# Three of the last mixture's four experts computed inside the attention's maxima pass, with the pass itself, list D and layer 0's edge terms rebuilt

## The chip, the cores and the metric

The kernel runs on one core of one Trainium2 chip. The metric is the device time of the execution in microseconds (us), the median of several runs. The core has five engines with a queue of instructions each: TensorE (PE; PEld is its weight load), VectorE (DVE), ScalarE (ACT), GpSimd (POOL) and SyncE (SP), which here only issues transfers. They wait for each other through semaphores.

## The reference, cut

Four stages on 6,250 nodes with 256 features, each added to its own input after a layer norm: a graph sum over 100,000 edges with a dense pair of layers, a mixture of eight experts, five graph layers with batch norm, and a last mixture of four experts whose shares come from graph attention. The change is about the last one.

```python
h = (x_flat @ W_gat).reshape(M, HEADS, NUM_EXPERTS)       # M = 6250 rows (the norm's batch is 1), 4 heads, 4 experts
src = concatenate([edge_index[0], loops]); dst = concatenate([edge_index[1], loops])   # 65,536 edges and a self loop each
a_src = (h * att_src).sum(-1);  a_dst = (h * att_dst).sum(-1)
e = leaky_relu(a_src[src] + a_dst[dst], 0.2)
ee = exp(e - segment_max(e, dst)[dst])
alpha = ee / (segment_sum(ee, dst)[dst] + 1e-16)
agg = segment_sum(h[src] * alpha[:, :, None], dst) + b_gat
scores = layernorm(agg).reshape(M, HEADS, NUM_EXPERTS).mean(1);  topk_s, topk_i = top_k(scores, 2)
for ei in range(NUM_EXPERTS):                              # every expert on every node, 256 -> 512 -> 256
    hh = gelu(x @ W1[ei] + b1[ei])
    out = out + g[..., None] * (hh @ W2[ei] + b2[ei])      # g: softmax weight where chosen, else 0
```

An expert's product needs no attention; only its share g does.

## The kernel before

Nodes are 49 tiles of 128 rows, in 7 groups of 7 tiles. The work is a list of phases, each ended by a barrier. The setup phase sorts three lists of edges by target tile on VectorE: A (first graph sum), C (the layers) and D (attention). List D has E2T = 561 columns of 128 edges, 512 of the 65,536 edges and 49 of self loops. A list is placed into DRAM by GpSimd's indirect scatters (L260), one a column. After placement the edges lie in chunks of 128 with one target tile each: NC2 = 624 for list D.

*The layers.* Five times, GpSimd gathers source rows with an indirect DMA for each chunk (L305), TensorE multiplies them with a one-hot matrix (L390), VectorE adds the bank to the tile's sum (L376). Behind its gathers of each layer GpSimd places a part of list D: 130 columns before the layers, 58 in each of layers 0 to 3, and the 199 that are left in layer 4. Layer 0 then adds the edges' own features for each of 14 half tiles: four f32 matmuls of 448 columns into the pair of banks own (L959), which wait until VectorE has added the pair before (L1012). The last layer's statistics end at L1053, and the barrier comes when GpSimd too is done.

*The last norm* (L618 to L671). Seven groups: load, normalise, turn to feature-major with TensorE, multiply with W_gat, copy the product (L647). SP first issues list D's load, then the norm's transfers.

*Attention*, first pass, the maxima. The table nodesD has 20 words a node: a_src of 4 heads and h. It is stored from row, and then 39 turns of 4 sets of 4 chunks run. For a set: ScalarE copies the indices (L1182), GpSimd gathers four times 128 rows (L305), ScalarE keeps them and makes 16 matrices of 128 by 128 with a_src on the diagonal (L1178), VectorE makes four matrices that hold a not-equal mask of the target (cold, L1277). TensorE writes, for each chunk, the row values spread over all partitions (ones times diag, f32, 512 columns, L1218) and minus 1e30 where the target differs (bf16, L1220) into a bank of 512 columns. Eight banks hold two sets. VectorE reduces four banks with one operation (L1288) and takes the maximum into the window's tile (L1295). TensorE is behind VectorE by its banks (the semaphore reduced). The second pass, the sums, takes the same rows from SBUF in 78 steps of 8 chunks. It gathers nothing.

*The last mixture* (class Ffn, also used for the first dense stage and the first mixture). The four experts' weights are loaded at its start, in about 10 us. For each group and expert TensorE makes 8 banks of up projections (L472, 32 matmuls), ScalarE the gelu (L506), TensorE 7 tiles of down projections (L485, 56 records), and VectorE adds the bias and the product, each times its share, to acc (L523, L527). Between two groups SP stores acc, waits for the store, and loads the next group's base into it:

```python
sp.wait_ge(self.stored, START + g * 16)
sp.dma_start(self.acc, group_rows(self.base, g)).then_inc(self.base_here, 16)
```

TensorE may run two experts ahead by its two hidden buffers, but only four tiles ahead by its y banks. With a single expert there is one hidden buffer.

## Time and profile before

| what | value |
|---|---|
| median of 3 runs | 15026.75 us (15017.78 to 15076.48) |
| the profiled execution, its own time | 15050.61 us |
| its span | 15048.9 us |
| granted TensorE clock, mean | 0.754 |
| busy: TensorE, weight load | 7919.9 us (53%), 5777.6 us (38%) |
| busy: VectorE, GpSimd, ScalarE | 6704.7 us (45%), 7539.6 us (50%), 1802.1 us (12%) |
| layers | 5110 to 12521 us |
| seam and last norm | 12521 to 12790 us |
| attention: start, maxima, sums, shares | 12797, 12826 to 13805, 13811 to 14330, to 14354 us |
| last mixture's experts | 14354 to 15049 us |

Times of stages are positions in the profiled execution, read off the timeline. Busy time is what an engine executes; the rest of its span it waits. The granted clock is a share of full speed: 0.50 is 1.2 GHz and 1.00 is 2.4 GHz.

### The profile page before, as it was taken

How to read it: one execution, taken by the hardware profiler on the slowest of the kernel's cores; microseconds unless marked ns; L12 is line 12 of the kernel's file. 1: busy time of each engine (PE TensorE's matmuls, PEld its weight loads, DVE VectorE, ACT ScalarE, POOL GpSimd, SP SyncE). 2: the span in 40 equal slices, each digit the busy share in tenths (PEclk: the TensorE clock that was granted, in tenths of full speed). 3: DMA queues.
4: the chain of work that ended last, by engine and by line, in shares of the span. 5: the costliest groups of instructions: out<-in, count | busy, mean ns of one | idle time of the engine just before them, and what ended most of it. 6: DMA issues, size and time to landing. Idle time of an engine off the chain costs nothing. (4 is left out here: it accounts for less than half of the span.)

```text
span 15048.9 us, 161728 instructions
## 1 busy us (share of the span) xinstructions
PE 7919.9 (53%) x35664; PEld 5777.6 (38%) x35704; DVE 6704.7 (45%) x18970; ACT 1802.1 (12%) x5161; POOL 7539.6 (50%) x7803
## 2 busy tenths in 40 slices
PE   0002455442139777656554655565556542676489
PEld 0002344331126544435443544444434442233356
DVE  7238544311015555544443444344434442566732
ACT  0000000000001100010001000100010001786211
POOL 5771566535750155545665666566656664563000
PEclk9999766675569888867666766677777665898599
DMA  1000222211000223213332333233323321100000
GB/s 56 18 1 0 76 85 85 71 43 43 2 6 20 84 80 80 80 56 85 86 86 70 86 86 87 69 86 86 86 68 85 86 75 36 8 7 4 0 30 17
DMA packets 483984, 833.28 MB, mean 55 GB/s; under 512 B 182276, under 2 KB 320821, under 8 KB 482869
## 3 DMA queue, kind: packets, MB, share of 16 engines
q0 software_dynamic: 327584, 673.89, 17.2%
q1 hardware_dynamic: 156309, 158.42, 3.3%
q8 instruction: 27, 0.44, 0.0%
q14 instruction: 64, 0.52, 0.0%
HBM read 751.88 MB, written 86.32 MB: 56 GB/s over the span
## 5 line engine op out<-in xcount | busy, mean ns | idle before, releaser
L305 POOL DMA_INDIRECT p_layers_place<-nodesC,p_layers_idx x4160 | 3945.7, 948 | 3033.1 <-issue 1593.1
L390 PE MATMUL p_layers_bank<-p_layers_hots,p_layers_place 128*128 128x128 f32 x16640 | 3440.7, 367 | 2872.0 <-DVE agg L376 1579.2
L390 PEld LDWEIGHTS p_layers_bank<-p_layers_hots,p_layers_place 128*128 128x128 f32 x16640 | 2927.3, 261 | 3471.1 <-issue 1858.6
L376 DVE TENSOR_TENSOR agg<-agg,p_layers_bank 128x256 f32 x4160 | 1752.1, 421 | 2445.0 <-issue 1052.1
L366 DVE TENSOR_SCALAR p_layers_hots<-iota,p_msg_edges 128x128 f32<-128x128 f32 x3328 | 995.7, 364 | 758.9 <-issue 581.9
L485 PE MATMUL p_ffn_y<-p_ffn_w,p_ffn_hid 128*128 128x256 f32 x3528 | 832.5, 396 | 724.0 <-issue 691.9
L305 POOL DMA_INDIRECT p_gather_rows<-xn,p_gather_idx x832 | 788.1, 947 | 838.3 <-ACT p_gather_idx L299 603.2
L260 POOL DMA_INDIRECT listC<-h x782 | 783.2, 1002 | 582.5 <-POOLq L1518 243.2
L485 PEld LDWEIGHTS p_ffn_y<-p_ffn_w,p_ffn_hid 128*128 128x128 f32 x3528 | 693.9, 198 | 874.6 <-issue 747.9
L260 POOL DMA_INDIRECT listA<-h x782 | 853.5, 1091 | 343.9 <-issue 238.8
L390 PE MATMUL p_agg_bank<-p_agg_hot,p_gather_rows 128*128 128x128 f32 x3328 | 695.0, 378 | 602.0 <-DVE agg L376 384.2
L299 ACT COPY p_layers_idx<-p_msg_edges 128x4 int32 x1040 | 203.1, 197 | 6418.2 <-PE p_layers_bank L390 2923.4
L390 PEld LDWEIGHTS p_agg_bank<-p_agg_hot,p_gather_rows 128*128 128x128 f32 x3328 | 611.6, 275 | 685.7 <-issue 448.1
L305 POOL DMA_INDIRECT gat_att_rows<-nodesD,gat_att_idx x624 | 590.9, 947 | 552.9 <-issue 183.7
L1218 PE MATMUL gat_att_banks<-gat_att_diag,ones 128*128 128x512 f32 x1248 | 709.2, 652 | 247.1 <-issue 127.8
L1178 ACT ACTIVATE gat_att_diag<-ident,gat_att_rows 128x128 f32<-128x128 f32 x2496 | 766.5, 388 | 166.7 <-issue 126.1
L260 POOL DMA_INDIRECT listD<-recD,rowD x561 | 552.9, 986 | 174.2 <-issue 174.2
L527 DVE SCALAR_TENSOR_TENSOR p_ffn_acc<-p_ffn_y,p_mix_share,p_ffn_acc 128x256 f32<-128x256 f32 x392 | 189.4, 483 | 960.3 <-remote 702.5
L376 DVE TENSOR_TENSOR agg<-agg,p_agg_bank 128x256 f32 x832 | 350.4, 421 | 454.2 <-issue 218.5
L472 PE MATMUL p_ffn_pre<-agg,p_ffn_w 128*128 x1120 | 454.8, 560 | 126.5 <-ACT p_ffn_hid L506 58.4
L506 ACT ACTIVATE p_ffn_hid<-p_ffn_pre,p_ffn_b 128x896 f32<-128x896 f32 x252 | 253.7, 1007 | 2150.5 <-PE p_ffn_pre L472 1025.8
L1288 DVE TENSOR_REDUCE gat_att_red<-gat_att_banks 128x16 f32<-128x2048 f32 x156 | 356.8, 2287 | 241.4 <-PE gat_att_banks L1220 101.4
(334 smaller groups left out, 7757.8 us busy)
## 6 DMA issues: line engine op xcount, KB each, us to landing
p_layers_place<-nodesC,p_layers_idx POOLq DMA_INDIRECT x4160
nodesC<-p_layers_place SPq DMA_DIRECT2D x24, 896.0 KB, 4.2
p_gather_rows<-xn,p_gather_idx POOLq DMA_INDIRECT x832
p_ffn_acc<-x SPq DMA_DIRECT2D x14, 896.0 KB, 5.2
x<-p_ffn_acc SPq DMA_DIRECT2D x14, 896.0 KB, 4.1
listA<-h POOLq DMA_INDIRECT x782
listC<-h POOLq DMA_INDIRECT x782
gat_att_rows<-nodesD,gat_att_idx POOLq DMA_INDIRECT x624
```

The source lines that it names most:

```text
L260: nc.gpsimd.indirect_dma_start(out=self.table, out_offset=bass.IndirectOffsetOnAxis(ap=self.row[0:n, t:t + 1], axis=0), in_=self.rec[0:n, ...
L299: nc.scalar.copy(self.idx[s], nodes).then_inc(self.ready[s], 1)
L305: nc.gpsimd.indirect_dma_start(out=self.rows[s][:, u, :], out_offset=None, in_=self.table, in_offset=bass.IndirectOffsetOnAxis(ap=self.idx ...
L366: ins = nc.vector.tensor_scalar(self.hot[s][:, u, :], self.sh.iota, place, weight, ALU.is_equal, ALU.mult)
L376: nc.vector.tensor_tensor(to, to, prod, ALU.add).then_inc(self.added[u], 1)
L390: ins = nc.tensor.matmul(self.bank[u][:, f * P:(f + 1) * P], self.g.rows[s][:, u, f * P:(f + 1) * P], self.hot[s][:, u, :], start=True, st ...
L472: ins = nc.tensor.matmul(self.pre[j][:, m, 0:HW], self.w1[:, e, f, b * P:(b + 1) * P], self.tok[:, f, ds(g * GW + m * HW, HW)], start=(f = ...
L485: ins = nc.tensor.matmul(self.y[j][:, 0:D], self.hid[e % self.nh][:, b, s * P:(s + 1) * P], self.w2[:, e * HB + b, :], start=(b == 0), sto ...
L506: nc.scalar.activation(self.hid[e % nh][:, b, :].rearrange("p (m n) -> p m n", m=2), self.pre[b % 2][:, :, 0:HW], self.func, bias=self.b1[ ...
L1178: ins = nc.scalar.activation(self.diag[s][:, u, a, :], sh.ident, ACT.Copy, scale=self.g.rows[s][:, u, a:a + 1])
L1218: nc.tensor.matmul(bank, sh.ones, self.diag[s][:, u].rearrange("p a n -> p (a n)"), start=True, stop=False)
L1288: nc.vector.tensor_reduce(red, self.banks[s % 2].rearrange("p u (a n) -> p u a n", a=HEADS), AX.X, ALU.max).then_inc(self.reduced, 1)
```

## The change

1. **Self loops leave list D.** E2T becomes 512 and NC2 560, so the maxima pass has 140 sets instead of 156 and the sums pass 70 steps instead of 78. The maxima start from each node's own a_src, and the sums from the self loop's exponential and its product with h, in a few whole-width operations ahead of the sums pass (one of them on ScalarE).
2. **Layer 0's edge terms** go into six single banks (the pair own, and four that the sums used), each with its own count, and VectorE adds one bank at a time.
3. **List D's tail.** The scatters left after layer 3, now 150 (512 less 130 less 4 times 58), leave layer 4 and run on GpSimd in the phase of the last norm. SP there loads the weights of three experts first (six loads of 512 KB), then serves the norm, and only then, when GpSimd has signalled the list, loads list D.
4. **The maxima pass** (class Tail instead of Attention). A table row has 26 words instead of 20: behind a_src and h stand three bf16 parts of a_src, which VectorE makes in four operations before the store. ScalarE copies a set's parts (thirds), TensorE turns them with one matmul of 128 columns against the identity into 48 rows, ScalarE writes them out by head in four operations (spreads), and for each chunk TensorE multiplies a selector with them: two bf16 matmuls of 512 columns a chunk, no f32 one. The 16 diagonal matrices a set are gone. The banks for it are 2 instead of 8, so VectorE reduces one chunk at a time, with a maximum for each.
5. **Three experts beside it.** The pass has 7 outer turns of 20 sets, one for each group of nodes. In a turn the 45 units of three experts (8 half banks of up projection and 7 tiles of down projection each) are dealt out to the 20 sets, 2, 2, 2 or 3 each. TensorE's order in a set is chunks 0 and 1, a unit, the turning of the next set, chunks 2 and 3, the other units. ScalarE does the gelu of each up unit and the copy of each down unit to keep; SP stores keep into part_y in DRAM. The bias b2 comes in by a bf16 matmul of three parts.
6. **The last mixture** computes one expert. At each group SP loads, behind the base, the three stored parts (896 KB each), and VectorE adds each of them times its share, tile by tile, before the expert's own sums.

```diff
-E2T = E2 // P + NT
+E2T = E2 // P
...
+TRI = 3 * HEADS
+GAW = AW + TRI // 2
+PAD_D = 24
...
-NC2 = chunks_of(E2 + NP)
+NC2 = chunks_of(E2)
...
+        self.old = [sp.sb(f"old{n}", [P, GT, D]) for n in range(len(parts))]
...
+            for old, (table, _) in zip(self.old, self.parts):
+                sp.dma_start(old, group_rows(table, g)).then_inc(self.base_here, 16)
...
-            dve.wait_ge(self.base_here, (g + 1) * 16)
+            dve.wait_ge(self.base_here, (g + 1) * (16 * (1 + len(self.parts))))
+            for n, (_, weight) in enumerate(self.parts):
+                for s in range(GT):
+                    a = self.acc[:, s, :]
+                    if n:
+                        dve.wait_ge(self.part_added, START + (g * len(self.parts) + n - 1) * GT + s + 1)
+                    nc.vector.scalar_tensor_tensor(a, self.old[n][:, s, :], weight[:, ds(g * GT + s, 1), 0], a,
+                                                   ALU.mult, ALU.add).then_inc(self.part_added, 1)
             for e in range(E):
...
+        self.edge_banks = [self.own[:, o, 0:HW] for o in range(FB)] + [bank[:, 0:HW] for bank in self.a.bank]
...
-            end = min(self.scat.T, at + PER_D) if l + 1 < LAYERS else self.scat.T
-            self.scat.pool(nc, pool, at, end)
-            at = end
-        self.scat.pool_done(pool)
+            if l + 1 < LAYERS:
+                self.scat.pool(nc, pool, at, at + PER_D)
...
         def edge(m):
-            pe.wait_ge(self.own_added, START + self.TILES + m)
             for o in range(FB):
-                ins = nc.tensor.matmul(self.own[:, o, 0:HW], self.ewm[:, o * P:(o + 1) * P],
-                                       self.agge[:, m * HW:(m + 1) * HW], start=True, stop=True)
-            ins.then_inc(self.own_done, 1)
+                n = m * FB + o
+                if n >= len(self.edge_banks):
+                    pe.wait_ge(self.edge_joined, START + n + 1 - len(self.edge_banks))
+                nc.tensor.matmul(self.edge_banks[n % len(self.edge_banks)], self.ewm[:, o * P:(o + 1) * P],
+                                 self.agge[:, m * HW:(m + 1) * HW], start=True, stop=True).then_inc(self.edge_made, 1)
...
+class Tail:
...
+    EARLY = 3
+    HB = 4
+    SETS = NC2 // U
+    PER = SETS // NG
+    UP, DOWN = 2 * HB, GT
+    UNIT = UP + DOWN
...
+        self.bank = [sp.ps(f"bank{h}", [P, 512]) for h in range(2)]
+        self.tr = sp.ps("tr", [P, 512])
+        self.pre = [sp.ps(f"pre{h}", [P, 512]) for h in range(2)]
+        self.y = [sp.ps(f"y{h}", [P, 512]) for h in range(2)]
...
+    def pieces(self, j):
+        total = self.EARLY * self.UNIT
+        return [divmod(n, self.UNIT) for n in range(j * total // self.PER, (j + 1) * total // self.PER)]
...
+        with sp.Fori(0, NG) as g:
+            for e in range(self.EARLY):
+                sp.wait_ge(self.y_kept, START + (self.unit(g, e) + 1) * GT)
+                hold(sp)
+                sp.dma_start(group_rows(self.ys[e], g), self.keep).then_inc(self.y_stored, 16)
+        sp.wait_ge(self.y_stored, START + NG * self.EARLY * 16)
...
+        def arrived(g, j):
+            k = g * self.PER + j
+            act.wait_ge(self.tr_done, START + k + 1)
+            act.wait_ge(self.spread, START + (k - 1) * U if not isinstance(k, int) or k else START)
+            for a in range(HEADS):
+                ins = nc.scalar.activation(self.spreads[j % 2][:, a, :], self.tr[0:self.R, 0:P], ACT.Copy,
+                                           scale=self.of_head[:, a:a + 1])
+            ins.then_inc(self.spread_ready, 1)
+        def lift(g, j):
+            k, s = g * self.PER + j, j % S
+            self.landed(act, g, j)
+            hold(act)
+            nc.scalar.copy(self.thirds[j % 2], self.rows[s][:, :, AW:GAW].bitcast(BF16)).then_inc(self.lifted, 1)
+            nc.scalar.copy(self.all[:, ds(k * U, U), :], self.rows[s][:, :, 0:AW]).then_inc(self.kept, 1)
+            nc.scalar.copy(self.idx[s], nodes((k + S) * U)).then_inc(self.ready[s], 1)
+        def experts(g, j):
+            for e, n in self.pieces(j):
+                at = self.unit(g, e)
+                if n < self.UP:
+                    b, m = divmod(n, 2)
+                    if n == 0:
+                        act.wait_ge(self.y_done, START + at * GT)
+                    act.wait_ge(self.pre_done, START + at * self.UP + n + 1)
+                    nc.scalar.activation(self.hid[:, b, m * HW:(m + 1) * HW], self.pre[n % 2][:, 0:HW], ACT.Gelu,
+                                         bias=self.b1[:, e * self.HB + b:e * self.HB + b + 1]).then_inc(self.gelu_done, 1)
+                else:
+                    t = n - self.UP
+                    if t == 0:
+                        act.wait_ge(self.y_stored, START + at * 16)
+                    act.wait_ge(self.y_done, START + at * GT + t + 1)
+                    nc.scalar.copy(self.keep[:, t, :], self.y[t % 2][:, 0:D]).then_inc(self.y_kept, 1)
...
+        def turn(g, last):
+            for j in range(self.PER):
+                if not (last and j + 1 == self.PER):
+                    arrived(g, j + 1)
+                experts(g, j)
+                if not last or j + 2 < self.PER:
+                    lift(g, j + 2)
...
+        def turn_rows(g, j):
+            k = g * self.PER + j
+            pe.wait_ge(self.lifted, START + k + 1)
+            if not isinstance(k, int) or k:
+                pe.wait_ge(self.spread_ready, START + k)
+            nc.tensor.matmul(self.tr[0:self.R, 0:P], self.thirds[j % 2].rearrange("p u w -> p (u w)"), self.ident,
+                             start=True, stop=True).then_inc(self.tr_done, 1)
+        def chunk(g, j, u):
+            k = g * self.PER + j
+            if u == 0:
+                pe.wait_ge(self.cold_ready, START + k + 1)
+                pe.wait_ge(self.spread_ready, START + k + 1)
+            pe.wait_ge(self.reduced, START + k * U + u)
+            bank = self.bank[u % 2]
+            nc.tensor.matmul(bank, self.cold[j % 2][:, u, :], self.off.rearrange("p a n -> p (a n)"), start=True,
+                             stop=False)
+            nc.tensor.matmul(bank, self.sel[:, u, :], self.spreads[j % 2].rearrange("p a n -> p (a n)"), start=False,
+                             stop=True).then_inc(self.spread, 1)
+        def up(g, e, n):
+            at, (b, m) = self.unit(g, e), divmod(n, 2)
+            if n == 0:
+                pe.wait_ge(self.gelu_done, START + at * self.UP)
+            else:
+                pe.wait_ge(self.gelu_done, START + at * self.UP + max(0, n - 1))
+            for f in range(FB):
+                ins = nc.tensor.matmul(self.pre[n % 2][:, 0:HW], self.w1[e][:, f, b * P:(b + 1) * P],
+                                       sh.h[:, f, ds(g * GW + m * HW, HW)], start=(f == 0), stop=(f == FB - 1))
+            ins.then_inc(self.pre_done, 1)
+        def down(g, e, t):
+            at = self.unit(g, e)
+            if t == 0:
+                pe.wait_ge(self.gelu_done, START + (at + 1) * self.UP)
+            pe.wait_ge(self.y_kept, START + at * GT + max(0, t - 1))
+            y = self.y[t % 2][:, 0:D]
+            nc.tensor.matmul(y, self.ones3, self.b2s[:, e, :], start=True, stop=False)
+            for b in range(self.HB):
+                ins = nc.tensor.matmul(y, self.hid[:, b, t * P:(t + 1) * P], self.w2[e][:, b, :], start=False,
+                                       stop=(b == self.HB - 1))
+            ins.then_inc(self.y_done, 1)
...
+        def turn(g, last):
+            for j in range(self.PER):
+                some = self.pieces(j)
+                chunk(g, j, 0)
+                chunk(g, j, 1)
+                for e, n in some[:1]:
+                    piece(g, e, n)
+                if not (last and j + 1 == self.PER):
+                    turn_rows(g, j + 1)
+                chunk(g, j, 2)
+                chunk(g, j, 3)
+                for e, n in some[1:]:
...
+        thirds = self.row[:, :, AW:GAW].bitcast(BF16)
+        link(nc.vector.tensor_copy(thirds[:, :, 0:HEADS], source))
+        link(nc.vector.tensor_tensor(rest, source, thirds[:, :, 0:HEADS], ALU.subtract))
+        link(nc.vector.tensor_copy(thirds[:, :, HEADS:2 * HEADS], rest))
+        nc.vector.tensor_tensor(thirds[:, :, 2 * HEADS:TRI], rest, thirds[:, :, HEADS:2 * HEADS],
+                                ALU.subtract).then_inc(self.rows_ready, 1)
...
+        def largest(g, j, last):
+            k = g * self.PER + j
+            if not last:
+                matrices(g, j + 1)
+            red = self.red[j % 2]
+            windows = windows_of(nc, mybir.EngineType.DVE, self.cw, k * U, U)
+            for u, w in enumerate(windows):
+                dve.wait_ge(self.spread, START + k * U + u + 1)
+                nc.vector.tensor_reduce(red[:, u, :], self.bank[u % 2].rearrange("p (a n) -> p a n", a=HEADS), AX.X,
                                         ALU.max).then_inc(self.reduced, 1)
-                windows = windows_of(nc, mybir.EngineType.DVE, self.cw, c, U)
-                dve.wait_ge(self.reduced, START + k + 3)
-                for u, w in enumerate(windows):
-                    dve.wait_ge(self.maxed, START + c + u)
...
+        dve.wait_ge(self.self_ex, START + 1)
+        nc.vector.tensor_copy(self.sums[:, :, 0:HEADS], self.low)
+        wide = self.low.rearrange("p t (a o) -> p t a o", o=1).to_broadcast([P, NT, HEADS, XD])
+        link(nc.vector.tensor_tensor(by_head(self.sums[:, :, HEADS:AW]), by_head(self.h16), wide, ALU.mult))
+        dve.wait_ge(self.kept, START + self.SETS)
...
+                            for e in range(Tail.EARLY):
+                                sp.dma_start(w1[e], L1_ffn_W1[e].rearrange("(f p) h -> p f h", p=P)).then_inc(here, 16)
+                                sp.dma_start(w2[e], L1_ffn_W2[e].rearrange("(b p) d -> p b d", p=P)).then_inc(here, 16)
+                            norm.sp(nc, sp)
+                            sp.wait_ge(listed, START + 1)
+                            hold(sp)
                             sp.dma_start(edges[:, 0:NC2, :].rearrange("p c w -> p (c w)"),
-                                         lanes(listD)).then_inc(here, 16)
-                            norm.sp(nc, sp)
...
+                            scatD.pool(nc, pool, PART_D + (LAYERS - 1) * PER_D, E2T)
+                            scatD.pool_done(pool)
+                            nc.gpsimd.sem_inc(listed, 1)
...
+            ffn = Ffn(space("ffn"), sh, sh.h, XD - Tail.EARLY, 4, L1_ffn_W1[late], L1_ffn_b1[late], L1_ffn_W2[late],
+                      L1_ffn_b2[late], ACT.Gelu, share[:, :, late], x3, out,
+                      parts=[(parts_y[e], share[:, :, e:e + 1]) for e in range(Tail.EARLY)])
```

## Rows read from the trace of the kernel before

**Rows 1.** Windows: length, PE/PEld/DVE/ACT/POOL busy (instructions), granted clock, DMA share, GB/s.
```profile
12826.00:13805.00 979.00, 766.84 (x1833) 312.44 (x1872) 596.24 (x1392) 790.82 (x2792) 582.37 (x615) 0.91 0.09 7
13811.00:14330.00 519.00, 216.50 (x3120) 175.00 (x3120) 373.75 (x1944) 146.89 (x195) 0.00 (x0) 0.50 0.00 0
14354.00:15048.00 694.00, 677.09 (x2464) 468.83 (x2464) 172.26 (x392) 121.77 (x119) 0.00 (x0) 0.99 0.08 25
```

**Rows 2.** Chain of waits, last stage: start, us, work.
```profile
14389.78 12.09 PE p_ffn_y L485 x56
14401.86 12.03 PE p_ffn_pre L472 x32
```

**Rows 3.** Groups by line and form, the maxima pass, largest first.
```profile
L1218 PE MATMUL gat_att_banks<-gat_att_diag,ones 128*128 128x512 f32 x1248 | 709.2, 652 | 247.1 <-issue 127.8 <-DVE gat_att_cold L1277 61.7 <-ACT gat_att_diag L1178 54.2
L305 POOL DMA_INDIRECT gat_att_rows<-nodesD,gat_att_idx x624 | 590.9, 947 | 552.9 <-issue 183.7 <-DMA nodesD<-gat_att_row 179.8 <-ACT gat_att_idx L1182 137.6
...
L1288 DVE TENSOR_REDUCE gat_att_red<-gat_att_banks 128x16 f32<-128x2048 f32 x156 | 356.8, 2287 | 241.4 <-PE gat_att_banks L1220 101.4 <-remote 90.0 <-issue 49.1
...
L1277 DVE TENSOR_SCALAR gat_att_cold<-iota,gat_in_edges 128x128 bf16<-128x128 f32 x624 | 146.2, 307 | 60.9 <-issue 53.1 <-DVE gat_att_sums L1270 0.2
...
L1295 DVE TENSOR_TENSOR gat_att_top<-gat_att_top,gat_att_red 128x4 f32 x624 | 102.9, 165 | 100.4 <-DVE gat_att_red L1288 12.3 <-issue 10.5
```

**Rows 4.** Line L305: min/median/max ns, first to last start.
```profile
L305 POOL DMA_INDIRECT p_gather_rows<-xn,p_gather_idx x832: 940/947/1018, 1561.7 to 2843.4; - x167
...
L305 POOL DMA_INDIRECT gat_att_rows<-nodesD,gat_att_idx x624: 939/945/1032, 12814.9 to 13778.0; - x156
```

**Rows 5.** Window of layer 0.
```profile
5175.00:6535.00 1360.00, 983.82 (x4981) 610.48 (x4979) 803.63 (x3466) 39.96 (x203) 774.15 (x814) 0.82 0.30 80
```

**Rows 6.** Timeline of GpSimd and VectorE, end of layer 4.
```profile
12367.75 1.00 POOL L260 DMA_INDIRECT listD<-recD,rowD  x1 [0.30 <-issue]
...
12492.65 0.42 DVE L376 TENSOR_TENSOR agg<-agg,p_layers_bank 128x256 f32 x1 [10.78 <-remote]
...
12521.30 0.16 DVE L1053 TENSOR_TENSOR shift<-p_layers_bn_b,p_layers_part 128x2 f32<-128x2 f32 x1 [0.55 <-DVE p_layers_part L1052]
...
12618.18 1.09 POOL L260 DMA_INDIRECT listD<-recD,rowD  x1 [0.30 <-issue]
12635.01 0.12 POOL L1886 MEMSET gat_in_edges<- 128x32 int32 x1 [15.73 <-POOLq L1841]
```

**Rows 7.** Timeline of VectorE, last two groups of the last norm.
```profile
12771.07 0.28 DVE L647 COPY gat_in_h<-gat_norm_prod 128x112 f32 x1 [7.24 <-PE gat_norm_prod L671]
...
12790.37 0.27 DVE L647 COPY gat_in_h<-gat_norm_prod 128x112 f32<-128x112 f32 x1 [7.13 <-PE gat_norm_prod L671]
```

**Rows 8.** Timeline of VectorE, first mixture's norm.
```profile
3550.64 0.22 DVE L647 COPY mix_router_logits<-mix_norm_prod 128x56 f32 x1 [96.92 <-remote]
...
3564.45 0.22 DVE L647 COPY mix_router_logits<-mix_norm_prod 128x56 f32 x1 [5.32 <-PE mix_norm_prod L671]
```

**Rows 9.** Window of the sort of list D.
```profile
1383.20:1548.60 165.40, 1.41 (x6) 1.16 (x6) 159.92 (x262) 0.00 (x0) 0.00 (x0) 1.00 0.00 0
```

**Rows 10.** Timeline of TensorE, layer 0's edge terms.
```profile
6680.45 3.35 PE L959 MATMUL p_layers_own<-rows,p_layers_ewm 4*128 4x448 f32 x4 [1.25 <-DVE agg L1012]
```

**Rows 11.** Timeline of TensorE, maxima pass.
```profile
12900.37 0.38 PE L1220 MATMUL gat_att_banks<-gat_att_off,gat_att_cold 128*128 128x512 bf16 x1
...
12900.58 1.02 PE L1218 MATMUL gat_att_banks<-gat_att_diag,ones 128*128 128x512 f32 x2
```

**Rows 12.** Timeline of TensorE, first dense stage, after a wait.
```profile
3204.12 8.69 PE L472 MATMUL p_ffn_pre<-agg,p_ffn_w 128*128 x16 [58.39 <-ACT p_ffn_hid L506]
```

**Rows 13.** Timeline of VectorE and SP, last stage, between two groups.
```profile
14462.22 0.48 DVE L527 SCALAR_TENSOR_TENSOR p_ffn_acc<-p_ffn_y,p_gat_share,p_ffn_acc 128x256 f32<-128x256 f32 x1 [0.85 <-PE p_ffn_y L485]
...
14467.29 0.39 SPq L444 DMA_DIRECT2D p_ffn_acc<-x  x1
...
14472.29 0.48 DVE L523 SCALAR_TENSOR_TENSOR p_ffn_acc<-p_ffn_b,p_gat_share,p_ffn_acc 128x256 f32<-128x256 f32 x1 [9.59 <-DMA p_ffn_acc<-x]
```

More of the change, by code:

```diff
@@ L1184, in keep_turned @@
+        turn(NG - 1, True)
+        act.wait_ge(self.self_low, START + 1)
+        nc.scalar.activation(self.low, self.low, ACT.Exp).then_inc(self.self_ex, 1)
         def keep_turned(k, h):
@@ new lines, in piece @@
+        def piece(g, e, n):
+            if n < self.UP:
+                up(g, e, n)
+            else:
+                down(g, e, n - self.UP)
+        def turn(g, last):
[10 more added lines that the diff above has]
+                for e, n in some[1:]:
+                    piece(g, e, n)
@@ L1224, in look_up @@
+        pe.wait_ge(self.consts, START + 3)
+        turn_rows(0, 0)
+        with pe.Fori(0, NG - 1) as g:
+            turn(g, False)
+        turn(NG - 1, True)
         def look_up(k, h):
@@ L1300, in dve @@
+        matrices(0, 0)
+        with dve.Fori(0, NG - 1) as g:
+            for j in range(self.PER):
+                largest(g, j, False)
+        for j in range(self.PER):
+            largest(NG - 1, j, j + 1 == self.PER)
         dve.wait_ge(self.maxed, START + NC2)
```

259 lines of the change are left out of this document (157 added, 102 removed).

## The prediction

> **What bounds the kernel now.** I read the busy shares by stage first. The end of the kernel is three stages: the maxima pass, 979 us at a granted clock of 0.91; the sums pass, 519 us at 0.50; the last mixture's experts, 694 us at 0.99 [rows 1]. In the last stage TensorE is busy 677 of 694 us, and the chain of waits alternates 12.03 us of up and 12.09 us of down projections without a gap: 24.12 us for one expert on one group, 28 such units, so 675 us [rows 2]. It is plain arithmetic, and TensorE bounds it.
>
> The maxima pass has no such owner. Of its 979 us TensorE is busy 767, ScalarE 791, VectorE 596, GpSimd 582 [rows 1], for 156 sets of four chunks: 6.28 us a set. The groups by line show what fills it [rows 3]: GpSimd issues four gathers at 0.95 us and 0.30 us between two (183.7 us of "issue" before 624), 5.0 us a set; no engine needs more than that on its own. What holds it is seen in the gathers' first and last start: 624 in 963 us is 1.546 us each, and the first aggregation, with rows of 1 KB and quite other engines' work, has 832 in 1282 us, 1.542 us [rows 4]. Two passes that share nothing but the indirect gathers run at one pace, a quarter above what GpSimd alone would take. Layer 0, whose TensorE and VectorE have the most to do per chunk, runs at 1.67 us (814 in 1360 us) [rows 5].
>
> Then the seam between the layers and the last mixture. GpSimd's last 199 list D scatters run from 12367.8 to 12618.2, 1.26 us each. Beside them VectorE's adds come every 11.2 us, each after 10.78 us idle, where they came at the gathers' pace before; the layer ends at 12521.3, and all wait for GpSimd until 12635.0 [rows 6]. The norm behind it needs 19.3 us a group undisturbed [rows 7]. The first mixture's norm, which has scatters beside it, shows what scatters do to it: 96.9 us idle before one copy, and 13.8 us for the next group once they were over [rows 8].
>
> **Part by part.** The sum is made against the profiled execution, 15050.6 us for a span of 15048.9; the median of the runs is 15026.75, 24 us (0.16%) lower, so the sum's difference is taken off the median.
>
> *Sort D.* From 1383.2 to 1548.6 only VectorE works, 159.9 us of it on 561 columns [rows 9]. 512 columns are 8.7% fewer. If all were per column that is 14 us, if nothing 0; I take -13.
>
> *Edge terms of layer 0.* TensorE 3.35 us and 1.25 us of waiting for VectorE, 4.60 us for each of 14 tiles [rows 10]. With more banks the wait goes. Records overlap a little, so I take 3.1 us a tile, -21 (3.35 gives -17; VectorE's two adds and two statistics, about half of 4.6, give -31).
>
> *List D's tail beside the norm.* Twelve adds at 11.2 us become twelve at the gathers' 1.55, so the last add moves from 12492.7 to about 12386; the 28.6 us to 12521.3, part of it held too, shrink to some 23: 12409. GpSimd starts 150 scatters (512 less the 362 placed by then) at 12411 and issues for 189 us, to 12600, and I give 11 us for landing. The norm starts meanwhile (19 us after GpSimd, as 7 x 19.3 back from 12790.4 gives 12655 against 12635; now behind 3 MB of weights) and is held: one group took 96.9 us and more in [rows 8], so 1.5 groups. The other 5.5 cost 106 us: 12717. List D's load, now behind the norm on SP, adds 6: 12723 against 12790. -67. Bounds: no group gets through, -38; the norm not held at all, end at 12617, -173. Its price without cover is thus the 189 us of issue.
>
> *Attention's start.* Four thirds operations, selectors and flags before the table store: +4 (0 to +8). What prepares the biases lies beside the store and the first gathers.
>
> *The maxima pass.* 140 sets now. TensorE per set: eight bf16 matmuls of 512 columns at 0.21 us (12900.37 to 12900.58, [rows 11]) make 1.7 us, the turning of the thirds 0.05, and 21 units of 24.12 us [rows 2] plus 7 bias matmuls of about 0.11 spread over 140 sets 3.7 us: 5.5 us at the higher clock, for some 23 matmul records a set instead of 12. VectorE: the reduction of 2287 ns becomes four of about 0.62 (a quarter, and a fixed part), with four maxima at 0.27 apart, four matrices at 0.22 and register loads: 5.0 us. ScalarE gives up 16 copies a set and takes four short ones, two evacuations and 2.25 pieces of the experts; it comes off the path. GpSimd stays at 5.0. Two chunks, a piece, two chunks, the rest is the order on TensorE; a piece of 1.5 to 1.8 us covers two reductions (1.3 us), so the pair of banks costs little. The gathers' own pace gives 6.2 us a set: the floor. The other end is 8.0: the dispatch of every engine is slowed while indirect DMAs run (the 10.78 us of [rows 6] is its extreme), and TensorE has twice the records. Layer 0's 6.67 is the nearest row, since there too TensorE is fullest. I take 6.7: 938 us, -41 (-111 at 6.2; +141 at 8.0). If TensorE waits and its clock sags to 0.91 as now [rows 1], 5.5 becomes 6.0, still inside.
>
> *The sums pass.* The self loops' exponentials and product ahead of it +4. 70 steps instead of 78 at 519/78 = 6.65 us: -53. Nothing in a step changes.
>
> *The last stage.* 694 us become seven groups of one expert. TensorE needs 24.1 us a group, but the group's chain is now longer. Now: last add at 14462.2, store, load at 14467.3, first add of the next at 14472.3, 10.1 us [rows 13]. Three more loads of 896 KB stand behind the first, which all must have landed: the first took 5.0 us from issue; I give the others 3.3 each (an estimate, two thirds of that, since four queued loads share the setting up), so 20.1 us from the last add. Then 21 operations of 0.48 us [rows 13], started 0.40 apart since they overlap, add the stored experts, 8.4; four waiting sums, then TensorE's last three tiles at 1.73 us (12.09 over 7), 6.8 in all: 35.3 us. TensorE waits some 10 us in each, and comes back slow: after a wait, 16 matmuls took 8.69 us [rows 12] where half of 12.03 would be 6.0. With part of those 2.7 us, 37 us a group. First group 37, six more 222, end 8: 267 us, -427. Bounds: loads hidden, TensorE's 24.1 and 1.4 for the last activation, 25.5 a group, -499; loads one after another at 5 us each and the full 2.7, 43 a group, -391.
>
> The Trainium skill, "TensorE: Matmul & The Clock Gate", section "HAM oscillation — how this bites in real kernels", says that waits for DMA between short bursts drop TensorE to the low clock again and again. The burst in [rows 12] agrees in kind. By the rule the clock drops at every group, 2.7 us at most each as that row has it, which would make the sum 7 us larger.
>
> Sum: -13 -21 -67 +4 -41 +4 -53 -427 = -614. 15026.75 - 614 = 14413 us.
>
> **Rivals.**
> *The gathers set the pace* (20%): 6.2 us a set, -111 instead of -41, and a norm that is held less, some -40 more. 14413 - 110 = about 14300. For it: two passes at one pace [rows 4]. Against: layer 0 [rows 5].
> *Dispatch holds the maxima pass* (20%): 8.0 us a set or more, because long unrolled bodies and twice the records are read while gathers run. +182: about 14595. For it: [rows 5, 6]. Against: TensorE streams the last stage's bodies without a gap [rows 2]. The Trainium skill, "Runtime: NRT & Kernel Launch", section "Instruction fetch mechanics", says that a taken branch to instructions no longer held costs a stall. By it each of the few jumps back would stall; no row here prices one.
> *The last stage stays at the low clock* (9%): TensorE needs 48 us a group, 7 x 48 + 17 = 353, +86: about 14500. For it: the 10 us waits; the sums pass stays at 0.50 [rows 1]. Against: the burst after each wait is 19 us long.
> *Slower* (4%): one mechanism, experts' matmuls at the low clock for the whole maxima pass. 5.5 us become 11.0, and with the quarter that the gathers' neighbourhood costs 12 to 13 us a set: 12.5 x 140 = 1750, +812 on the forecast, 15225. It decides from 11.1 us a set on (6.7 + 614/140). Against: the clock is 0.91 in this pass at 78% busy, and the share rises.
> *No effect that can be told* (2%): a set between 10.6 and 11.1 us.
>
> **Numbers.** Forecast 45%, with 14340 to 14490 as its own range; gathers' pace 20%, dispatch 20%, low clock 9%, slower 4%, none 2%. A measurement of this kernel can tell about 0.5% (75 us) from no change. Range 14250 to 14630: it takes the first rival whole, with the better bounds of the norm and the last stage, and the second with 0.2 us a set more. Faster 94%, same 2%, slower 4%.
>
> **What would show it.** Right: the last stage near 267 us with VectorE waiting for the loads at each group; the maxima pass near 940 us, GpSimd at about 1.65 us a gather, clock above 0.9; the norm's groups stretched to near 100 us until the scatters end, then 19.3 us; the sums pass at 465 us; edge tiles 3.1 us apart. Wrong: gathers more than 2 us apart, last-stage groups not near 37 us, or a norm that runs on beside the scatters. The estimate stands or falls with the set time of the maxima pass, 140 us for each microsecond.

## The result

The changed kernel took 14470.85 us, median of 4 runs (14433.16 to 14485.11), beside 15022.26 us for the kernel before: a ratio of 0.962 (95% interval 0.9604 to 0.9635), 551 us less. The forecast was 614 less, 14413 us, with 14250 to 14630 as the range. The profiled executions differ by more, 15048.9 against 14431.4, 617.5 us; the table shows where most of the other 66 come from.

| from, to | before | after | difference | forecast |
|---|---|---|---|---|
| list D's sort, first operation to last | 166.8 | 154.9 | -12 | -13 |
| layer 0's last gather to its shift | 156.9 | 137.0 | -20 | -21 |
| that shift to the last gather of layer 4 | 5672.8 | 5626.1 | -47 | 0 |
| last gather of the layers to the norm's last copy | 423.9 | 340.8 | -83 | -67 |
| to the attention's first gather | 24.5 | 30.6 | +6 | +4 |
| first gather to the last maximum | 992.7 | 1015.2 | +23 | -41 |
| last maximum to the last sum | 524.6 | 474.4 | -50 | +4 -53 |
| last sum to the end | 716.7 | 279.2 | -438 | -427 |

These are first and last starts of the lines concerned (in the first row, to the end of the last operation), in the one profiled execution of each kernel.

The windows of the same three stages after, the kinds of column as in [rows 1]:

```profile
12663.00:13678.00 1015.00, 961.91 (x3180) 459.61 (x3244) 543.99 (x1673) 369.95 (x1305) 528.89 (x560) 0.98 0.16 26
13693.00:14155.00 462.00, 191.26 (x2783) 155.01 (x2781) 335.73 (x1732) 86.94 (x139) 0.00 (x0) 0.50 0.00 0
14183.00:14431.00 248.00, 187.40 (x616) 125.97 (x616) 101.76 (x245) 37.19 (x35) 0.00 (x0) 0.89 0.40 127
```

TensorE is now the owner of the maxima pass: 962 of 1015 us at 0.98, where it had 767 of 979 in [rows 1], a window that starts 11 us behind the first gather. That is 6.9 us a set of 140; I had summed 5.5. The timeline of TensorE there shows the difference:

```profile
13101.46 0.39 PE L1362 MATMUL gat_att_bank<-gat_att_spreads,gat_att_sel 48*128 48x512 bf16 x1
13101.78 0.39 PE L1360 MATMUL gat_att_bank<-gat_att_off,gat_att_cold 128*128 128x512 bf16 x1
13102.10 0.39 PE L1362 MATMUL gat_att_bank<-gat_att_spreads,gat_att_sel 48*128 48x512 bf16 x1
13102.42 0.28 PE L1382 MATMUL gat_att_y<-gat_att_b2s,gat_att_ones 3*128 3x256 bf16 x1
13102.63 1.99 PE L1384 MATMUL gat_att_y<-gat_in_w,rows 128*128 128x256 f32 x8
13104.55 0.24 PE L1350 MATMUL gat_att_tr<-gat_att_ident,gat_att_thirds 128*48 128x128 bf16 x1
13104.72 0.39 PE L1360 MATMUL gat_att_bank<-gat_att_off,gat_att_cold 128*128 128x512 bf16 x1
```

The bf16 matmuls of 512 columns start 0.32 us apart, not 0.21 as the one in [rows 11]. They alternate between weights of 128 rows and of 48. A down unit takes 2.13 us from its bias to the turning (12.09/7 = 1.73 in [rows 2]).

The chain of waits between two groups of the last stage:

```profile
14211.32 0.49 DVE p_ffn_acc L544
14212.06 4.11 DMA out_dram<-p_ffn_acc
...
14218.07 11.21 DMA p_ffn_old<-part_y
...
14238.90 7.18 PE p_ffn_y L493 x24
14246.11 0.50 DVE p_ffn_acc L544
```

Store 4.1 us, 11.2 us from the issue of the fourth load until all four have landed, the adds, then TensorE's last three tiles, 6.9 to 8.5 us in the six groups: 34.8 us here, 36.2 for the next group, 35.4 on average. I had 37. TensorE waits 7.3 to 7.6 us in each group.

VectorE in the last norm, to compare with [rows 7, 8]:

```profile
12458.68 0.28 DVE L664 COPY gat_in_h<-gat_norm_prod 128x112 f32 x1 [109.14 <-remote]
12534.95 0.28 DVE L664 COPY gat_in_h<-gat_norm_prod 128x112 f32 x1 [29.93 <-PE gat_norm_prod L688]
12554.50 0.27 DVE L664 COPY gat_in_h<-gat_norm_prod 128x112 f32 x1 [7.24 <-PE gat_norm_prod L688]
```

GpSimd's 150 scatters of list D beside it:

```profile
L263 POOL DMA_INDIRECT listD<-recD,rowD x150: 954/959/1013, 12319.3 to 12507.7; - x150
```

VectorE idles 109 us before the first group's copy, and the second group's copy comes only after the last scatter; from there on the pace is 19.5 us.

### The profile page after: what moved, and what is told of

Same layout as the page of the kernel before. It is cut to its first block and busy times, and to the rows that moved or that the text cites. A ratio compares the mean times of both kernels' runs of the same rounds, so it can differ in the third digit from the quotient of the medians.

```text
span 14431.4 us, 158805 instructions
## 1 busy us (share of the span) xinstructions
PE 7588.0 (53%) x34855; PEld 5559.9 (39%) x34919; DVE 6539.3 (45%) x18932; ACT 1235.6 (9%) x3524; POOL 7427.6 (51%) x7692
## 5 line engine op out<-in xcount | busy, mean ns | idle before, releaser
L493 PE MATMUL p_ffn_y<-p_ffn_w,p_ffn_hid 128*128 128x256 f32 x2352 | 591.9, 412 | 773.4 <-issue 682.7
L493 PEld LDWEIGHTS p_ffn_y<-p_ffn_w,p_ffn_hid 128*128 128x128 f32 x2352 | 478.9, 207 | 897.3 <-issue 735.5
L1248 POOL DMA_INDIRECT gat_att_rows<-nodesD,gat_att_idx x560 | 529.2, 945 | 480.7 <-ACT gat_att_idx L1278 269.6
L263 POOL DMA_INDIRECT listD<-recD,rowD x512 | 504.7, 986 | 159.5 <-issue 159.5
L1509 DVE TENSOR_REDUCE gat_att_red<-gat_att_bank 128x4 f32<-128x512 f32 x560 | 376.1, 689 | 419.5 <-PE gat_att_bank L1362 245.2
L365 DVE SCALAR_TENSOR_TENSOR p_layers_hots<-iota,p_msg_edges,p_msg_dinv_row 128x128 f32<-128x128 f32 x832 | 275.0, 353 | 267.5 <-issue 186.3
L396 PE MATMUL p_layers_bank<-p_layers_hots,p_layers_attr 128*4 128x128 f32 x1664 | 359.2, 303 | 0.0
```

Source lines behind the costliest of these rows:

```text
L263: nc.gpsimd.indirect_dma_start(out=self.table, out_offset=bass.IndirectOffsetOnAxis(ap=self.row[0:n, t:t + 1], axis=0), in_=self.rec[0:n, ...
L365: ins = nc.vector.scalar_tensor_tensor(self.hot[s][:, u, :], self.sh.iota, place, self.by[:, ds(windows[u] * P, P)], ALU.is_equal, ALU.mul ...
L396: ins = nc.tensor.matmul(self.bank[u][0:4, D:D + P], self.attr[s][:, u, :], self.hot[s][:, u, :], start=True, stop=True)
L493: ins = nc.tensor.matmul(self.y[j][:, 0:D], self.hid[e % self.nh][:, b, s * P:(s + 1) * P], self.w2[:, e * HB + b, :], start=(b == 0), sto ...
L1248: nc.gpsimd.indirect_dma_start(out=self.rows[s][:, u, :], out_offset=None, in_=self.table, in_offset=bass.IndirectOffsetOnAxis(ap=self.idx ...
L1509: nc.vector.tensor_reduce(red[:, u, :], self.bank[u % 2].rearrange("p (a n) -> p a n", a=HEADS), AX.X, ALU.max).then_inc(self.reduced, 1)
```

## The experiments

Each kernel is the changed one with the edit shown. The first four and the second four ran beside a kernel before of 14857 and 14916 us. The last four ran on a chip on which it took 11764 us, for a reason that no run here settles; ratios are always within one chip, and times of stages from there are marked as such.

The runs no_experts, one_gather, two_early, tail_in_layer4, edge_two_banks, rows_banks_one_gather and all_rows have one execution each. Their whole times are not compared: with the same instructions ahead of them, the layers' first gather starts at 4999 us in tail_in_layer4 and at 5095 in edge_two_banks, so most of the difference between their 14224 and 14338 us lies outside the edits. Stages are compared instead.

On the first two chips the maxima pass as in the changed kernel ran three times more, in kernels whose edit is elsewhere: 1006.8 us (parts_ahead), 1008.1 (tail_in_layer4) and 1007.4 (edge_two_banks), with TensorE busy 969 to 971. These, and not the 1015 of the first profile, are the measure for runs on their chips.

**Padding the selector** (sel_rows).

```diff
-        self.spreads = [sp.sb(f"spreads{j}", [self.R, HEADS, P], BF16) for j in range(2)]
-        self.sel = sp.sb("sel", [self.R, U, P], BF16)
+        self.spreads = [sp.sb(f"spreads{j}", [P, HEADS, P], BF16) for j in range(2)]
+        self.sel = sp.sb("sel", [P, U, P], BF16)
...
+        link(nc.vector.memset(self.sel, 0.0))
...
```

Both spreads are set to zero too; rows 0 to 47 are written as before.

> The selector and the spread rows are padded with zeros from 48 to 128 partitions; nothing else changes. In the changed kernel the bf16 matmuls of 512 columns start 0.32 us apart in the maxima pass, where in the kernel before one took 0.21 us, and their weight loads start together with them instead of ahead. Theory R (a change in the number of rows, 128 to 48 and back, keeps the next weights from being loaded ahead): they come 0.21 us apart, TensorE needs about 0.9 us less of its 6.9 us a set, the pass falls from about 1007 us to between 870 and 890 us (the gathers' 6.2 us a set or TensorE's 6.1), and the kernel is 110 to 140 us faster than the changed one. Theory D (TensorE's dispatch beside gathers, or its semaphores, sets the 0.32 us): spacing and pass stay, within 10 us.

The timeline of TensorE:

```profile
12999.68 0.38 PE L1360 MATMUL gat_att_bank<-gat_att_off,gat_att_cold 128*128 128x512 bf16 x1
12999.89 0.38 PE L1362 MATMUL gat_att_bank<-gat_att_spreads,gat_att_sel 128*128 128x512 bf16 x1
```

The window of the pass:

```profile
12598.00:13569.00 971.00, 876.71 (x3247) 463.51 (x3247) 540.01 (x1674) 369.45 (x1305) 530.74 (x560) 0.97 0.17 27
```

0.21 us apart: theory R. TensorE's need falls from 969 us (parts_ahead, same chip) to 877, the pass only from 1007 to 970; the kernel's ratio is 0.9588 (0.957 to 0.9606), whose interval still touches that of the changed kernel. The expectations that the pass would reach 890 us, and the kernel gain 110 us or more, failed. Something else holds it at 970.

**The pass without experts** (no_experts: `pieces` returns an empty list, no stored parts, the last mixture has one expert) and **one gather of four** (one_gather: `for u in range(1)` around the gather, the wait adapted, the other rows zero). Both leave work out, so neither computes the reference.

> Leaves out the three experts altogether: no units in the maxima pass, no stored parts, the last mixture computes and adds only the fourth expert. Theory T (TensorE bounds the maxima pass, 965 of 1007 us busy): without its 4.3 us a set of experts the pass falls to the pace of the gathers, 6.2 us a set, 870 us. Theory G (the gathers or the dispatch of short instructions set the 7.2 us a set): it stays above 960 us. The last stage without stored parts: about 25.5 + 6 us a group, 190 to 215 us instead of 248.

> Each set gathers only its first chunk of 128 rows; the other three chunks' rows are zeros written once, so the maxima and sums are not those of the reference. Theory T (TensorE's own instructions are 6.9 us a set, whatever the gathers do): the pass stays at 960 to 1000 us. Theory G (indirect transfers stretch every engine's instructions): 7.2 falls to TensorE's 5.5 us as I had summed it from undisturbed rows, the pass to 770 to 850 us. A fall of some 30 us only would be the stalls of 5 to 10 us at long intervals.

The window of the pass without experts:

```profile
12520.00:13429.00 909.00, 647.08 (x1260) 131.34 (x1260) 561.15 (x1674) 211.00 (x981) 530.10 (x560) 0.50 0.13 9
```

With one gather:

```profile
12521.00:13503.00 982.00, 966.00 (x3245) 457.98 (x3246) 539.63 (x1674) 369.96 (x1305) 131.78 (x140) 0.99 0.08 21
```

Without three quarters of the gathers TensorE is busy 966 of 982 us: theory T, the work itself is 6.9 us a set, and three of four gathers cost the changed kernel 25 us only (1007 to 982). Without experts the pass is 908 us, between the 870 of theory T and the 960 of theory G, and TensorE, which is busy 647 of 909 us, is granted 0.50, the level of 1.2 GHz. The run thus takes away the experts and lowers the clock at once, and what holds it at 908 us is not shown. The last stage took 189 us, its six groups 25.5 us each: TensorE's own need.

**Loading the stored parts ahead** (parts_ahead).

```diff
             sp.dma_start(self.acc, group_rows(self.base, g)).then_inc(self.base_here, 16)
-            for old, (table, _) in zip(self.old, self.parts):
-                sp.dma_start(old, group_rows(table, g)).then_inc(self.base_here, 16)
+            if self.parts and not last:
+                sp.wait_ge(self.part_added, START + (g + 1) * (len(self.parts) * GT))
+                hold(sp)
+                load_parts(g + 1)
...
+        load_parts(0)
...
```

> In the last stage the three stored parts of the next group are loaded as soon as VectorE has added this group's, instead of behind the store and the base. Now a group has 4.1 us of store, 11.3 us of four loads, 8.4 us of adds and about 8 us of TensorE's last tiles on its chain, 35 to 36 us. Theory L (the four loads are on the chain): the load falls to the 5 us of one, six groups give 35 to 40 us. Rival: the three loads collide with nothing but the chain is held by TensorE, then no more than 10 us.

The chain of waits from one group's last add to the next's:

```profile
14086.51 0.49 DVE p_ffn_acc L551
...
14112.07 0.49 DVE p_ffn_acc L551
14112.81 5.35 DMA out_dram<-p_ffn_acc
14118.38 5.01 DMA p_ffn_acc<-x
```

The window of the stage:

```profile
14058.00:14253.00 195.00, 174.13 (x616) 116.85 (x616) 101.77 (x245) 37.19 (x35) 0.00 (x0) 0.98 0.50 163
```

195 us instead of 248, 53 less, more than the 35 to 40 expected. From one group's last add to the next's are now 25.6 us in the group shown, nearly the 25.5 that I had given TensorE as its own need, and 26.5 to 26.9 in the other five, whose chain is still the store, the base's load and the adds. TensorE's waits are now 1.1 us, and its granted clock is 0.98 instead of 0.89. Ratio 0.9582 (0.9565 to 0.9599).

**Everything padded, three banks, parts ahead** (rows_banks_ahead). Ones and bias thirds also get 128 rows, and `self.bank[(j * U + u) % 3]` takes the eighth bank.

> Selector, spread rows, ones and bias thirds padded to 128 partitions, a third bank for the maxima's chunks, and the stored parts loaded ahead in the last stage. With the padding of the selector alone TensorE was busy 876 of 958 us and waited 54 us for VectorE's reductions. Theory R and B (the two banks are what is left): the bias rows save 0.1 us for each of three down and some up units a set, the third bank the 54 us; the pass ends at the gathers' pace, 890 to 915 us, 100 us and more below the changed kernel's 1015, and with the last stage at 195 us the kernel is 140 to 170 us faster than the changed one, a ratio to the kernel before near 0.951. Rival (stalls of 5 to 10 us beside the gathers are what is left): no better than 950 us.

**Two experts beside the pass** (two_early: `EARLY = 2`).

> Two experts beside the maxima pass instead of three, two in the last stage. TensorE's work a set falls from 6.9 to about 5.5 us. Theory T (TensorE bounds the pass at 6.9 us, the gathers at 6.3): the pass ends near 900 us, as without any expert (908 us from first gather to last maximum), 110 us below the 1015 of three; the last stage is bound by TensorE at 48.2 us a group, 7 x 48.2 and some 12 us, about 350 us instead of 248: together 10 to 15 us faster than the changed kernel. Rival (the pass is held by something else than TensorE's work): pass above 960 us, and the kernel slower by 50 us or more.

The window of the pass with three banks:

```profile
12484.00:13470.00 986.00, 851.02 (x3248) 472.71 (x3249) 539.21 (x1674) 369.66 (x1306) 530.31 (x560) 0.95 0.17 27
```

With two experts:

```profile
12492.00:13472.00 980.00, 849.37 (x2586) 361.64 (x2587) 541.31 (x1672) 317.35 (x1201) 530.67 (x560) 0.91 0.15 21
```

Both expectations of the pass failed. Less work on TensorE takes it from 1008 us to 986 and 980 only, with more idle time and a lower granted clock. The rival of each was nearer: on the first two chips three kernels with experts in the pass, TensorE busy 849 to 877 us, end at 970 to 986 us. It is no floor of the gathers alone, since the pass without experts took 908. Two experts cost 348 us in the last stage, from its first matmul to the end, as summed, where three leave 248; by these stages two lose some 70 us to three. The whole kernel with three banks has a ratio of 0.9559 (0.9538 to 0.958), not the 0.951 expected, and its interval overlaps that of parts_ahead (0.9565 to 0.9599), whose edit it contains. A gain of the whole kernel from the padding and the bank is not shown there.

**The scatters back in layer 4** (tail_in_layer4: `end = min(self.scat.T, at + PER_D) if l + 1 < LAYERS else self.scat.T`, as before).

> One part undone: the 150 last scatters go back behind layer 4's gathers; the weights of three experts and the list's late load stay. From layer 4's shift to the attention's first gather the changed kernel takes 345 us. My sum had the move at -67 us against 199 scatters; the profile after says -83 from the last gather of the layers to the end of the norm. Theory M (scatters beside other work cost about as much as alone, the gain is only the part of layer 4's end and of the norm that gets through): with 150 scatters back, last gather to the norm's end is 150 x 1.26 + 17 + 155 = 360 to 385 us instead of 341, 20 to 45 us longer; most of the 83 us were the 49 scatters less. Rival (the move itself is the gain): 400 us and more.

The layers' gathers, first to last start:

```profile
L308 POOL DMA_INDIRECT p_layers_place<-nodesC,p_layers_idx x4160: 943/949/1071, 4998.8 to 12066.1; - x199
```

The norm's last copy, from the timeline:

```profile
12428.79 0.28 DVE L664 COPY gat_in_h<-gat_norm_prod 128x112 f32<-128x112 f32 x1 [7.13 <-PE gat_norm_prod L688]
```

362.7 us from one to the other, against 340.8 after and 423.9 before. So 61 of the 83 us are the 49 scatters that no longer exist, at 1.26 us each, and the move itself gave 22 (17 to 22, since the same stretch took 340 to 346 us in the other kernels that have the move): theory M.

**Two single banks for the edge terms** (edge_two_banks: `edge_banks` only from `own`).

> Layer 0's edge terms in two single banks instead of six; the adds stay one bank each. My sum gave the six banks -21 us, from 4.6 to 3.1 us for each of 14 tiles. If TensorE's and VectorE's alternation is what cost 4.6 us, two single banks give between 3.4 and 4.6 us a tile, 4 to 20 us more from the last gather of layer 0 to its end; if VectorE's adds are the bound, nothing changes.

VectorE's adds with two banks, first to last start:

```profile
L1043 DVE TENSOR_TENSOR agg<-agg,p_layers_own x28: 601/620/622, 6542.0 to 6582.3; 128x448 f32<-128x448 f32 x28
```

The changed kernel has them in two groups:

```profile
L1043 DVE TENSOR_TENSOR agg<-agg,p_layers_bank x18: 601/620/623, 6623.5 to 6660.3; 128x448 f32<-128x448 f32 x18
L1043 DVE TENSOR_TENSOR agg<-agg,p_layers_own x10: 602/620/623, 6622.0 to 6657.3; 128x448 f32<-128x448 f32 x10
```

The kernel before has 14 adds, each of a pair of banks:

```profile
L1012 DVE TENSOR_TENSOR agg<-agg,p_layers_own x14: 1086/1087/1089, 6628.7 to 6688.5; 128x896 f32<-128x896 f32 x14
```

And the changed kernel's matmuls:

```profile
L981 PE MATMUL p_layers_bank<-rows,p_layers_ewm x36: 534/949/949, 6622.5 to 6659.3; 4*128 4x448 f32 x36
L981 PE MATMUL p_layers_own<-rows,p_layers_ewm x20: 534/949/949, 6621.0 to 6656.3; 4*128 4x448 f32 x20
```

40.3 us with two, 38.3 with six, 59.8 with the old pair. The -20 us are right, but they come from giving each bank its own count, not from having more banks. With six banks TensorE waits for no add, while VectorE waits 10.9 us for TensorE: the 56 matmul records, 0.70 us apart, are the bound, 2.8 us a tile where I had taken 3.1. With two banks each waits 14 to 16 us for the other, and the stretch is 2 us longer.

**The changed kernel again, and the best version** (after_again; sel_ahead is padding of the selector and parts ahead), on the chip where the kernel before took 11764 us.

> The changed kernel as it is, beside the best version. What it is for: layers 1 to 3 took 1428.5 us each in the profile after and 1443.8 in the one before, with the same instructions. If that is the execution and not the change, the time from the layers' first to last gather moves by tens of us here too, while the maxima pass (1015 us), the sums (474 us) and the last stage (248 us) stay within 10 us.

> The selector and the spread rows padded to 128 partitions, and the stored parts loaded ahead; two banks, bias thirds in 3 rows as in the changed kernel. If the two gains add up, the maxima pass takes 970 us and the last stage 195 us, 95 to 100 us less than the changed kernel on the same chip, a ratio of 0.993 to it and near 0.955 to the kernel before. If the third bank and the full bias rows did help in the run that had them, this one is slower than that one (0.9559).

| kernel | median, 5 runs | ratio to before |
|---|---|---|
| after_again | 11263.01 | 0.9573 (0.956 to 0.9586) |
| sel_ahead | 11102.16 | 0.9436 (0.9423 to 0.9449) |

Here the layers do not move: layers 1 to 4 take 1115 to 1118 us each in all four kernels profiled on this chip, and the maxima pass of after_again is 990 us, not within 10 us of 1015. So the run does not tell why the layers differed on the first chips. sel_ahead is 161 us faster than after_again, not 95 to 100: its last stage is the 195 us expected, its pass 884 instead of 970. Its comparison with the 0.9559 of another chip says nothing of the third bank.

**All rows padded**, once with one gather and three banks (rows_banks_one_gather), once with all gathers and two banks (all_rows), on the same chip.

> All rows padded to 128 and three banks, and each set gathers only its first chunk; the rows of the other three chunks are zeros, so the maxima and sums are not those of the reference. With all gathers this kernel's pass took 986 us with TensorE busy 851. Theory S (stalls beside the gathers make the rest): without them the pass falls to TensorE's own need, about 6.0 us a set, 845 to 880 us. Theory C (the fixed order of pieces on TensorE and ScalarE, a chain of its own, makes the rest): it stays above 930 us.

> Selector, spread rows, ones and bias thirds padded, two banks. Tells what of the 986 us with three banks, against 970 with the selector alone, is the third bank. If the third bank does nothing but let TensorE run ahead into gaps, 965 to 990 us here too; if the third bank hurts, 955 to 965.

The window of the pass on this chip, changed kernel:

```profile
9517.00:10507.00 990.00, 955.19 (x3181) 457.69 (x3245) 543.35 (x1673) 369.96 (x1305) 529.00 (x560) 0.99 0.17 27
```

sel_ahead:

```profile
9508.00:10392.00 884.00, 846.36 (x3182) 461.59 (x3246) 536.86 (x1673) 369.33 (x1305) 529.03 (x560) 0.99 0.20 30
```

all_rows:

```profile
9517.00:10361.00 844.00, 806.78 (x3180) 461.12 (x3244) 538.11 (x1670) 370.01 (x1305) 530.21 (x560) 0.99 0.21 31
```

rows_banks_one_gather:

```profile
9513.00:10349.00 836.00, 806.26 (x3182) 462.29 (x3246) 531.79 (x1672) 369.40 (x1305) 132.10 (x140) 0.99 0.10 25
```

Here the theory of the rows shows undiluted: 990, 884 with the selector padded, 844 with the bias rows too, TensorE the bound in all. Taking away three of four gathers and adding a bank changes 844 to 836. So the order of the pieces (theory C) is no floor of its own. That the 970 to 986 us of the first chips come from gathers that disturb the others, as theory S has it, fits, but is not shown: shown is that they are absent on this chip, where the gathers run undisturbed; one gather with all rows padded was not run on the first chips. Whether the third bank hurts, the question of all_rows, has no answer for the same reason.

## Why the prediction was right

*Right, mechanism and size.* The sort (-12 of -13), the edge terms (-20 of -21, though by the split counts), self loops and sums (-50 of -49), the last stage (-438 of -427; 35.4 us a group of 37). With the loads ahead a group fell to 25.6 to 26.9 us, near the lower bound of 25.5. The clock is 0.89 in this stage with waits of 7.5 us and 0.98 with those of 1.1. The Trainium skill, "TensorE: Matmul & The Clock Gate", section "HAM oscillation — how this bites in real kernels", has waits between bursts bring the low clock; these two windows agree in kind. The last three tiles after each wait took 6.9 to 8.5 us where three at 1.73 us are 5.2, so 1.7 to 3.3 us more; [rows 12] had 2.7. This is inside the 35.4 us.

*Right, size off.* List D's tail, -83 for -67. The norm was held as forecast: from the first of the 150 scatters to its last copy are 312.7 us, where the sum had 189 + 11 + 106 = 306 and 6 more for the list's load. What was mis-sized is the end of layer 4: from its last gather to the first scatter 28.1 us instead of the 44.5 of the sum (12366.5 to 12411). My text had it as one piece of scheduling; tail_in_layer4 divides it into 61 us for fewer scatters and 22 for the move.

*Wrong: the term of the maxima pass.* It came out at +23 us instead of -41. The step that failed is "eight bf16 matmuls of 512 columns at 0.21 us", which should "make 1.7 us", and with it "21 units of 24.12 us". [Rows 11] has a bf16 matmul between f32 ones, all with weights of 128 rows; I carried its time to matmuls that alternate between 128, 48 and 3 rows. Measured: 8 x 0.32 = 2.56, the turning 0.17, and 21 x (8 x 1.70 + 7 x 2.13)/140 = 4.28, in all 7.0 us a set for the 5.5 forecast (busy time says 6.9). sel_rows shows the cause, all_rows its size: 990 - 845 = 145 us, or 1.0 us a set. The other 0.4 us are not the rows: with all of them padded, an up unit still takes 1.60 us up to the next matmul and a down unit 1.93, where [rows 2] gives 1.50 and 1.73 (1.84 with its bias), and the turning 0.17 where I had 0.05. The sum had put these turns between units and chunks at nothing. The set as a whole, 7.2 us against 6.7, was closer than its largest part because I had taken the value from layer 0, which is disturbed by the gathers, and the two errors covered each other.

So of the signs that I had named, the pass near 940 us and the gathers at 1.65 us did not come true (1015, and 1.76 from the first gather's start at 12662.6 to the last's at 13644.5). The total stayed inside the range because this miss of 64 us was small beside the 438 us of the last stage.

*The rivals.* The gathers' pace (6.2 us a set) did not decide, since TensorE needed more. Dispatch at 8 us did not either. The low clock did not hold the pass with experts (0.98), and the last stage only in part (0.89, between the two levels); no_experts shows it at 0.50 where TensorE has 647 of 909 us of work. The rival on the other side needed 11.1 us a set and is excluded by the same windows.

*Not in the sum.* Layers 1 to 3 took 1443.8 us each before and 1428.0 after with the same instructions. Between executions on one of the first chips the same layers took 1406 (no_experts) to 1434 us (parts_ahead), a wider spread. So the 47 us are not shown to be the change's, nor shown not to be, with one profile of the kernel before, and the medians, 551 us apart, are the better measure. Of the stages of the table, which make 574 without them, the maxima pass is 64 us above its forecast and the others together 24 below theirs; the remaining 23 us lie between profiled executions and medians.

## What to carry to other kernels

A duration carries over only with its neighbours: a matmul's cost between others of the same row count is not its cost between others of another count, so look at start-to-start times in a stream of the same mix. Padding a short operand with zeros can be free, or a gain. And once the bound is relieved, the next one is met at once: the padded selector took 92 us off TensorE's work and 37 off the pass on one of the first chips, and 109 and 106 on the last.

## What the runs showed of the hardware that I had not expected

- Between bf16 matmuls of 128 and of 48 rows, 512 columns each, a start takes 0.32 us instead of 0.21, and the weight load is recorded together with its matmul (13102.10 both) instead of ahead of it (in sel_rows the load starts at 12999.68, its matmul at 12999.89). Selector and spread rows were padded together, so which of the two operands counts is not separated. An up unit of four f32 matmul records takes 1.70 us up to the next matmul, and 1.60 with the selector padded, where four of the last stage's take 4 x 0.376 = 1.50.
- The same changed kernel takes 14471 us on one chip and 11263 on another. The other's layers, again first and last gather:

```profile
L308 POOL DMA_INDIRECT p_layers_place<-nodesC,p_layers_idx x4160: 940/947/1073, 3700.3 to 9266.0; - x199
L308 POOL DMA_INDIRECT p_gather_rows<-xn,p_gather_idx x832: 942/947/1022, 1299.4 to 2341.0; - x167
```

  The 832 gathers of the first aggregation take 1042 us there, 1.25 us each, GpSimd's own issue, where [rows 4] had 1282 us. In the norm all seven groups run at 19.2 to 19.6 us beside the scatters, and VectorE's 109 us of idle time is absent. What I had read as the price of indirect transfers in this kernel, their pace and the slow dispatch beside them, is thus met on the first chips only. Its cause is open.
- On both chips the last stage (248 and 249 us) and the sums (474 us) are the same, so it is the stages beside gathers and scatters that differ.
